# Householder tridiagonalisation of a 512 x 512 Laplacian: two dots in one sum, the step's vector operations reordered, and the pivot row summed early in the last block

## The reference, cut to what matters

```python
deg = jnp.sum(A, axis=0) + jnp.sum(A, axis=1) - jnp.diagonal(A)
d_inv_sqrt = jnp.where(deg > 0, jax.lax.rsqrt(deg), 0.0)
L = jnp.diag(deg) - A
L_norm = d_inv_sqrt[:, None] * L * d_inv_sqrt[None, :]
_, U = jnp.linalg.eigh(L_norm)
agg = jnp.einsum('mn,bnd->bmd', U.T, features)
h = jax.nn.relu(agg @ W1 + b1)
out = h @ W2 + b2
return jnp.einsum('nm,bmd->bnd', U, out)
```

## Time and profile before

| what | value |
|---|---|
| median of 3 runs | 5796.45 us (5794.7 to 5798.84) |
| the profiled execution | 5797.87 us, of it the profiled span 5796.2 us |
| busy: PE, PEld | 3847.7 us (66%), 2559.1 us (44%) |
| busy: DVE, ACT | 4287.2 us (74%), 1342.6 us (23%) |
| mean granted TensorE clock | 0.655 of 2.4 GHz |
| from the first x to the last (L297 to L404) | 47.3 to 2522.5 us |

### The profile page before, as it was taken

One profiled execution on the slowest core, in us unless ns is written; L12 is line 12 of the kernel. 1 busy time (PEld: TensorE's weight loads), 2 busy tenths in 40 slices (PEclk: granted clock), 3 DMA queues, 4 the chain that ended last, 5 costly groups with the idle time before them and its releaser, 6 DMA issues. The chain is left out here.

```text
span 5796.2 us, 63099 instructions
## 1 busy us (share of the span) xinstructions
PE 3847.7 (66%) x12287; PEld 2559.1 (44%) x12287; DVE 4287.2 (74%) x24282; ACT 1342.6 (23%) x5439; POOL 51.2 (1%) x82
## 2 busy tenths in 40 slices
PE   5889998898777777754445444441056687885757
PEld 5777777777655566641112111220033343322334
DVE  7999988888888877789999999999923312223354
ACT  1222222222322333310000000000002225333444
POOL 0000000000000000000000000000000000000000
PEclk6555555555555555567677677665568898997979
DMA  0000000000000000000000000000010000000000
GB/s 8 1 1 1 1 1 1 1 1 1 1 1 1 1 1 1 1 1 0 0 1 0 0 0 0 0 1 0 0 38 12 0 0 0 0 0 0 0 9 20
DMA packets 14148, 16.01 MB, mean 3 GB/s; under 512 B 571, under 2 KB 10214, under 8 KB 13798
## 3 DMA queue, kind: packets, MB, share of 16 engines
q1 hardware_dynamic: 13798, 12.48, 0.8%
HBM read 8.28 MB, written 4.19 MB: 2 GB/s over the span
## 5 line engine op out<-in xcount | busy, mean ns | idle before, releaser
L552 DVE RECIPROCAL sturm_recip<-sturm_pivots 128x32 f32<-128x32 f32 x2560 | 713.8, 320 | 0.0
L550 DVE SCALAR_TENSOR_TENSOR sturm_pivots<-sturm_recip,neg_e,ps 128x32 f32<-128x32 f32 x2560 | 470.3, 203 | 29.3 <-PE ps L502 29.3
L277 ACT ACTIVATE vectors<-V,refl 128x4 f32<-128x4 f32 (+3 forms) x511 | 152.6, 299 | 1218.0 <-DVE refl L394 1218.0
L510 PE MATMUL ps<-sturm_flags,ident_flags 128*128 128x512 bf16 x160 | 82.7, 621 | 522.8 <-ACT sturm_flags L525 522.8
L219 PE MATMUL ps<-dot_part,ones 128*128 128x1 f32 x766 | 224.3, 362 | 271.8 <-DVE dot_part L389 271.4
L219 PEld LDWEIGHTS ps<-dot_part,ones 128*128 128x128 f32 x766 | 191.6, 311 | 428.9 <-DVE dot_part L389 428.9
L208 PE MATMUL ps<-ident,vectors 128*128 128x128 f32 x1148 | 341.9, 435 | 33.3 <-DVE vectors L404 4.7
L1236 PE MATMUL ps<-h_features,WihT 128*128 x504 | 296.0, 747 | 49.3 <-ACT gates_skip L1267 28.3
L525 ACT ACTIVATE sturm_flags<-sturm_pivots,pivot 128x1024 bf16<-128x1024 f32 x80 | 91.8, 1148 | 1007.1 <-DVE pivots_mark L555 953.1
L501 PE MATMUL ps<-points,ident 128*128 128x512 f32 x320 | 250.8, 879 | 63.5 <-DVE points_mark L536 63.5
L510 PEld LDWEIGHTS ps<-sturm_flags,ident_flags 128*128 128x128 bf16 x160 | 10.5, 110 | 589.2 <-ACT sturm_flags L525 589.2
(11 more groups left out here) (461 smaller groups left out, 9356.9 us busy)
## 6 DMA issues: line engine op xcount, KB each, us to landing
out_dram<-x SPq DMA_DIRECT2D x16, 256.0 KB, 2.3
adj<-in_adj_dram SPq DMA_DIRECT2D x1, 1024.0 KB, 5.3
l2w_in<-in_L_gnn_W_dram SPq DMA_DIRECT2D x2, 128.0 KB
Wqkv<-in_L_gnn_Wqkv_dram SPq DMA_DIRECT2D x1, 192.0 KB
L_gnn_W<-in_L_gnn_W_dram SPq DMA_DIRECT2D x2, 64.0 KB
L_gnn_Wg<-in_L_gnn_Wg_dram SPq DMA_DIRECT2D x2, 64.0 KB
x<-in_x_dram SPq DMA_DIRECT2D x4, 0.5 KB
L_gnn_Wo<-in_L_gnn_Wo_dram SPq DMA_DIRECT2D x1, 64.0 KB
```

The costliest lines, as they stand in the source:

```text
L550: r.inc(nc.vector.scalar_tensor_tensor(out=S,in0=R,scalar=neg_e2[:,row+dr:row+dr+1],in1=XD[h%2][dr][:,slot],op0=ALU.mult,op1=ALU.add))
L552: r.inc(nc.vector.reciprocal(R,S))
```

## The change

In `tridiagonalise`, and in the helpers that say when tiles are updated:

- **One sum for both dots.** V.y and V.cc are two L389-like operations into `dp[:,0:2]`, summed by one matmul (`dots`). kappa = S (V.cc) + V.y is one operation. L221, L328 and L329 go.
- **Scalars.** The copy of the squared norm (L274) goes. One three-fold reciprocal of two products (L370, L371) and A1 (L359) becomes a reciprocal of N2 = S (S + alpha) and S; x_scaled multiplies by two column scalars at once. In blocks 1 to 3 V is made of `hs` = sub times sign and of T2.
- **Order.** p moves from ahead of the next x to behind it (`close`, blocks 0 to 2). y is made ahead of cc in blocks 0 to 2, behind it in block 3. The reciprocal, the sign, T2 and the corrections have an order of their own in each block. Where an instruction waits for several semaphores, the waits come in another order.
- **Sums.** For m < 256 the norm and the pairs' dots are one matmul over `gp`, behind ROWS; from 256 on the norm's sum waits for kappa and no longer for w.
- **Last block.** The pivot's row for step m+1 is summed behind the dot of step m, from bu and p. Its entry for w is then put in by VectorE in PSUM (`KAPH`, `row_at`). bu is made by VectorE there.
- **Updates.** One tile a step at most. In blocks 0 and 1 a step with an update has no product on TensorE, and VectorE multiplies all columns. Blocks 2 and 3 take the new version after 4 and 3 steps, not 2. ScalarE copies the updated tile ahead of its wait for beta (`u_ready`).

```diff
+def panel_lag(p): return (5,4,4,3)[panel_block(p)]
+def update_from(p): return (1,1,2,2)[panel_block(p)]
 def version(m):
...
+    p=m//PANEL-1
+    if p<0: return None
+    t=panel_block(p)+m%PANEL-update_from(p)
+    return (p,t) if m%PANEL>=update_from(p) and t<NT else None
+def products(m):
+
+    return sum(1 for q in range(1,m+1) if pe_tiles(q))
+def pe_tiles(m):
+
+    b=m//P
+    if b==NT-1: return range(NT-1,NT)
...
-                        nc.tensor.matmul(NORM[:,0:1],ones[:],nrm[:],start=True,stop=True).then_inc(s2_ps,1)
-                        nc.tensor.matmul(ROWS[:,X_:hi],at,XG[:,b,X_:hi],start=True,stop=True).then_inc(sel_ps,1)
-                        if L:
+                        if m>=SEP:
+                            pe.wait_ge(nrm_ready,m); pe.wait_ge(kap_ready,m-1)
+                            nc.tensor.matmul(NG[:,0:1],ones[:],gp[:,0:1],start=True,stop=True).then_inc(s2_ps,1)
+                        if m>1: pe.wait_ge(ub_ready,m-1); pe.wait_ge(w_ready,m-1)
+                        nc.tensor.matmul(ROWS[:,X_:last_slot(m)],pivot(m),XG[:,b,X_:last_slot(m)],start=True,stop=True).then_inc(sel_ps,1)
+                        if m<SEP:
+                            pe.wait_ge(nrm_ready,m)
+                            if m>1: pe.wait_ge(kap_ready,m-1); pe.wait_ge(gp_ready,m-1)
+                            nc.tensor.matmul(NG,ones[:],gp[:],start=True,stop=True).then_inc(s2_ps,1)
+                        else:
                             pe.wait_ge(gp_ready,m-1)
-                            nc.tensor.matmul(by_kind(gdot(m))[:,:,L[0]:L[1]],ones[:],gp[:,:,L[0]:L[1]],start=True,stop=True).then_inc(g_ps,1)
+                            nc.tensor.matmul(pair_dots(m),ones[:],halves(gp),start=True,stop=True).then_inc(g_ps,1)
...
-                        nc.tensor.matmul(DOT[:,0:1],ones[:],dp[:],start=True,stop=True).then_inc(dot_ps,1)
-                        pe.wait_ge(c_ready,m)
-                        nc.tensor.matmul(AT,at,XG[:,b,Y_:Y_+2],start=True,stop=True).then_inc(at_ps,1)
+                        nc.tensor.matmul(dots(m),ones[:],dp[:],start=True,stop=True).then_inc(dot_ps,1)
...
+                        if m==TAIL: pe.wait_ge(kap_ready,m-1)
+                        nc.tensor.matmul(NG[:,0:2],xx,XG[:,NT-1,E_:X_+1],start=True,stop=True).then_inc(s2_ps,1)
+                        pe.wait_ge(ub_ready,m-1); pe.wait_ge(w_ready,m-1)
+                        nc.tensor.matmul(pair_dots(m)[:,:,L[0]:L[1]],xx,by_kind(XG[:,NT-1,:])[:,:,L[0]:L[1]],start=True,stop=True).then_inc(g_ps,1)
...
+                        nc.tensor.matmul(dots(m),V[:,NT-1,m-1:m].broadcast_to([P,P]),XG[:,NT-1,Y_:Y_+2],start=True,stop=True).then_inc(dot_ps,1)
+                    if TAIL<=m+1<N:
+                        pe.wait_ge(ub_ready,m); pe.wait_ge(pc_ready,m)
+                        nc.tensor.matmul(ROWS[:,PC_:last_slot(m+1)],pivot(m+1),XG[:,NT-1,PC_:last_slot(m+1)],start=True,stop=True).then_inc(sel_ps,1)
...
                         act.wait_ge(x_ready,m)
-                        nc.scalar.activation(sq[:,u,sl],XG[:,sl,X_],ACT.Square,accum_out=nrm[:]).then_inc(nrm_ready,1)
-                    if m>PANEL and m%PANEL==1: rows_copied(m//PANEL-1)
+                        nc.scalar.activation(sq[:,2,sl],XG[:,sl,X_],ACT.Square,accum_out=gp[:,0:1]).then_inc(nrm_ready,1)
+                    if new_rows and m<SEP: rows_copied(m//PANEL-1)
                     act.wait_ge(s2_ps,m)
...
                     if TAIL<=m+1<N: nc.scalar.copy(XG[:,NT-1,E_:E_+1],ident[:,(m+1)%P:(m+1)%P+1]).then_inc(e_ready,1)
+                    if not wide:
+                        act.wait_ge(h_ready,m-TAIL+1)
+                        nc.scalar.activation(hs[:,sl],sub[:,sl,i],ACT.Copy,scale=s[:,u,H:H+1]).then_inc(hs_ready,1)
+                    if new_rows and m>=SEP: rows_copied(m//PANEL-1)
+                    if update_tile(m): tile_copied(*update_tile(m))
                     act.wait_ge(u_ready,m)
-                    nc.scalar.activation(XG[:,sl,U_],V[:,sl,i],ACT.Copy,scale=s[:,u,T0:T0+1]).then_inc(ub_ready,1)
+                    if wide: nc.scalar.activation(XG[:,sl,U_],V[:,sl,i],ACT.Copy,scale=s[:,u,T0:T0+1]).then_inc(ub_ready,1)
+                    act.wait_ge(ub_ready,m)
+                    nc.scalar.activation(ubh[:,sl],XG[:,sl,U_],ACT.Copy,scale=-0.5).then_inc(ubh_ready,1)
                     nc.scalar.copy(tau[:,i:i+1],s[:,u,T0:T0+1]).then_inc(kept,1)
                     nc.scalar.copy(esub[:,i:i+1],s[:,u,S_:S_+1]).then_inc(kept,1)
-                    act.wait_ge(ub_ready,m)
-                    nc.scalar.activation(ubh[:,sl],XG[:,sl,U_],ACT.Copy,scale=-0.5).then_inc(ubh_ready,1)
-                    for p,t in updated_tiles(m): tile_copied(p,t)
...
+                def close(q):
+
+                    w=q%2; sl=slice(q//P,NT); early=TAIL<=q+1<N
+                    col=lambda j: s[:,w,j:j+1]
+                    v.wait_ge(dot_ps,q)
+                    nc.vector.scalar_tensor_tensor(out=col(KAP),in0=col(S_),scalar=dots(q)[:,1:2],in1=dots(q)[:,0:1],op0=ALU.mult,op1=ALU.add).then_inc(kap_ready,1)
+                    if q<TAIL: p_col(q)
+                    v.wait_ge(ubh_ready,q)
+                    if q>=PANEL and q%PANEL==0: v.wait_ge(gt_ps,q//PANEL)
+                    v.wait_ge(pc_ready,q)
+                    if early:
+                        v.wait_ge(kap_ready,q)
+                        k.inc(nc.vector.tensor_scalar(col(KAPH),col(KAP),-0.5,None,ALU.mult)); half_at=k.at()
+                        v.wait_ge(sel_ps,q+1)
+                    v.wait_ge(kap_ready,q)
+                    nc.vector.scalar_tensor_tensor(out=XG[:,sl,G_+SPREAD+slot(q)],in0=ubh[:,sl],scalar=col(KAP),in1=XG[:,sl,PC_],op0=ALU.mult,op1=ALU.add).then_inc(w_ready,1)
+                    if early:
+                        v.wait_ge(ds,half_at)
+                        k.inc(nc.vector.scalar_tensor_tensor(out=ROWS[:,G_+SPREAD+slot(q):G_+SPREAD+slot(q)+1],in0=col(KAPH),scalar=ROWS[:,G_+slot(q):G_+slot(q)+1],in1=ROWS[:,PC_:PC_+1],op0=ALU.mult,op1=ALU.add)); row_at[0]=k.at()
+                def p_col(q):
+                    sl=slice(q//P,NT)
+                    v.wait_ge(y_ready,q); v.wait_ge(c_ready,q)
+                    nc.vector.scalar_tensor_tensor(out=XG[:,sl,PC_],in0=XG[:,sl,C_],scalar=s[:,q%2,S_:S_+1],in1=XG[:,sl,Y_],op0=ALU.mult,op1=ALU.add).then_inc(pc_ready,1)
...
+                        if b==0:
+                            after("S")
+                            mark("V",nc.vector.scalar_tensor_tensor(out=V[:,sl,i],in0=sub[:,sl,i],scalar=col(S_),in1=x,op0=ALU.mult,op1=ALU.add))
+                        else:
+                            if wide: after("T2","hs")
+                            else: v.wait_ge(hs_ready,m-TAIL+1); after("T2")
+                            mark("V",nc.vector.scalar_tensor_tensor(out=V[:,sl,i],in0=hs[:,sl],scalar=col(T2),in1=x,op0=ALU.mult,op1=ALU.add))
...
+                    def dot_parts():
+                        v.wait_ge(y_ready,m); after("V")
+                        k.inc(nc.vector.tensor_tensor_reduce(out=sq[:,0,sl],in0=V[:,sl,i],in1=y,scale=1.0,scalar=0.0,op0=ALU.mult,op1=ALU.add,accum_out=dp[:,0:1]))
+                        v.wait_ge(c_ready,m)
+                        nc.vector.tensor_tensor_reduce(out=sq[:,1,sl],in0=V[:,sl,i],in1=cc,scale=1.0,scalar=0.0,op0=ALU.mult,op1=ALU.add,accum_out=dp[:,1:2]).then_inc(dp_ready,1)
+                    def denominator():
+                        after("S")
+                        mark("N2",nc.vector.scalar_tensor_tensor(out=col(N2_),in0=col(S_),scalar=ALPHA,in1=col(S_),op0=ALU.add,op1=ALU.mult))
...
+                        after("xym"); v.wait_ge(u_ready,m)
+                        mark("xt",nc.vector.tensor_scalar(xt[:,sl],xym[:,sl,0],col(T0),col(Q),ALU.mult,ALU.mult))
...
+                        if L:
+                            v.wait_ge(ub_ready,m-1); v.wait_ge(x_ready,m); v.wait_ge(w_ready,m-1)
+                            link(nc.vector.tensor_tensor(prod[:,sl,:,0:n],pairs(),x.unsqueeze(2).unsqueeze(3).broadcast_to([P,NB,2,n]),ALU.mult))
+                            nc.vector.tensor_reduce(halves(gp)[:,:,L[0]:L[1]],prod[:,sl,:,0:n].rearrange("p t e s -> p e s t"),AX.X,ALU.add).then_inc(gp_ready,1)
+                        v.wait_ge(A_copied,copies_of(version(m))); v.wait_ge(xrow_ps,m)
+                        if b==0:
+                            multiply(2); inverse(); sign(); multiply(1); twice_norm(); multiply(2)
+                            by_dots(); by_rows(); shift(); add_product(); corrections(); reflector()
+                            matrix_times_x(); column_of_A()
+                        elif b==1:
+                            multiply(3); sign(); inverse(); signed_sub(); by_dots(); twice_norm(); by_rows()
+                            add_product(); corrections(); reflector()
+                            matrix_times_x(); column_of_A(); shift()
+                        else:
```

(54 more changed lines are left out.)

201 lines of the change are left out of this document (61 added, 140 removed).

## The result

The changed kernel takes 5712.14 us (median of 4 runs, 5709.32 to 5713.75), the kernel before, beside it, 5795.57 (4 runs, 5794.57 to 5798.84): a ratio of 0.9855 [0.9843, 0.9868]. The change saves 83 us where I had forecast 179; the range, 5555 to 5700, does not hold the result. The profiled execution took 5713.75, its span 5712.1, and the mean granted clock was 0.656 (0.655 before).

The account below looks back on a forecast made before the run. In the 511 Householder steps VectorE's chain of tiny dependent operations was taken as the bound, with some TensorE waits. Blocks 0 to 3 gain 35 + 44 + 67 + 33 = 179 us, giving 5618 us, range 5555 to 5700.

Parts of the forecast that it names:

- the price of the hand-overs behind several waits: Between dependent operations: w to prod 0.28 us with the blocking wait last; 0.03 for two waits ahead of x.
- Block 2: Steps of block 2: 0.48 us a step from front and middle less a longer tail, plus update-step effects; 67 us.
- The tail of 1.32: Block 2, from y to the next x: 1.32 us against 1.29 before, with the second dot and x_scaled added.
- Block 0: Steps of block 0: 0.25 us a step over 127 steps, and 3 us for the rest; 35 us.
- the update steps would come out even: Block 0's update steps: VectorE's full last tile, at most 0.4 us more, offset by an addition dropped and an earlier update.
- Block 1: Steps of block 1: 0.27 us a step, 35 us, plus 9 us in update steps; 44 us.
- Block 3: Steps of block 3: y at 2.02 to 2.05 us after x, x at 3.16; 0.26 a step, 33 us.
- The covers: Blocks 0 and 1, ScalarE: the updated tile's copy is done at 4.5 us, ahead of beta near 5.
- Only the number of operations counts: Rival for all steps: VectorE operations at 0.2 us each, less longer update-step products; gain 39 us, 5759; chance 0.05.
- The gates in blocks 0 and 1: Rival: w or the parts 0.3 us later hold the root; blocks 0 and 1 gain nothing; 5698 us; chance 0.12.
- The clock: Slower rival, stages behind the steps: TensorE granted under 0.77; at 0.70, 180 us longer, at 0.67, 5890; chance 0.03.
- the one with 0.04: Rival, no change: waits put their issue time on the chain, 0.35 us a step, leaving 5797; chance 0.04.

Follow-up runs that it names:

- experiment 1: The changed kernel with the wait that ends last moved to the front of each list, except at KAPH; same operations: 5622.3 us, ratio to before 0.9695.
- experiment 2: The changed kernel with the two waits ahead of x exchanged, so that y_scaled's, which ends last, is written second: 5745.49 us.
- Experiment 4: The changed kernel with the last tile's product back on TensorE in update steps too, in blocks 0 and 1: 5701.77 us.
- experiment 6: From experiment 1, block 3's pivot row summed behind the pairs' dots of its own step, without KAPH and the entry set in PSUM: 5660.56 us.
- experiments 1 and 7: The second of these: from experiment 1, x_scaled multiplied by one column scalar, leaving out 1/S, so output isn't the reference's: 5593.37 us.

## Why the prediction was wrong

**The step that failed** is the price of the hand-overs behind several waits. Where the prediction names it, in the front of a step, it says: "From w to prod it was 0.31, more than a link of 0.25; with the blocking wait last I take 0.28". I took a late wait at the end of the list for the cheaper place. It is the dear one: 0.35. At x_scaled, at S of block 3 and behind the transposes the prediction added nothing for the waits and took a bare link. The table has the distance from the start of an operation to the start of the one that waits for it, by the place of that wait in the source:

| place of the late wait | seen at | start to start, us |
|---|---|---|
| first | x behind y_scaled; w to prod in experiment 1 | 0.25; 0.26 |
| middle of three | w to prod before; p to w after | 0.31; 0.31 |
| last of three; last of two | w to prod after; x behind y_scaled in experiment 2 | 0.35; 0.31 |

The change wrote the late wait last at prod, the first product, x_scaled, by_rows, KAPH and S of block 3 and, on TensorE, the joined sum and the pairs' dots of block 3. Moving all of them but KAPH's (experiment 1) was worth 90 us. It left 4 of the 94 us between my forecast and the result, the net of 9 us that block 2 had over and what the other blocks lacked.

**Block 2** (67 forecast, 47 measured, 76 in experiment 1). Taken over the 16 steps with m mod 8 = 6, prod is at 0.95, the first product 1.29, y 2.86 and x 4.20 in the changed kernel (forecast 0.83, 1.17, 2.72, 4.04) and at 0.81, 1.15, 2.73 and 3.99 in experiment 1. The middle is right to 0.02. The tail of 1.32 measured 1.34, but by two errors: x stands 0.25 behind y_scaled and not 0.28, and x_scaled 0.27 behind the reciprocal and not 0.21, with its late wait last. The turn behind an update gave 9 us (forecast 11), and the longer pending pairs took 4 (forecast 5).

**Block 0** (35, 12, 32.5). The steps of block 0 with m mod 8 = 6, from step 17 on, fell from 5.73 to 5.64, 0.09 where 0.25 was laid out, and to 5.46 in experiment 1. Products behind the transposes began at 1.55 (1.46 before): the first product has its late wait last, 0.15 behind the end of the transposes (1.40), and 0.04 behind it in experiment 1. Here "the earlier w gains nothing" was right and hid a loss. The tail measured 1.42, not 1.32: with four columns the dots are 0.12 apart and the first stands 0.15 behind cc. That the update steps would come out even held, from step 17 on: they gained 0.14, 0.09, 0.11 and -0.02. Experiment 4 shows that it was a poor standard, since with the product on TensorE three of them are 0.25 to 0.31 shorter.

**Block 1** (44, 16, 43). The steps with m mod 8 = 6 stayed as they were, 4.85 and 4.87, and are 4.63 in experiment 1. The steps with m mod 8 from 1 to 4, the update steps and the one behind them, gave nearly the whole gain, 15.9 of 16.2 us (forecast for update steps 9). The joined sum's weight load begins 0.12 behind the parts (1.50 after 1.38) and the reciprocal comes at 2.48, 0.09 behind the end of the products; in experiment 1 these are 0.05, 2.31 and 0.03. The tail holds S as well (the order of block 1 puts it behind y), which I had left out: 1.44.

**Block 3** (33, 5.5, 23.5). KAPH, the pairs' dots and S, as shown above. What experiment 1 lacks in this block, 9.5 us, has the size of KAPH's hand-over: it stands 0.34 behind kappa where a link is 0.25, so w starts at 0.59 and not at 0.52, and 0.07 a step would be 9 us. In experiment 1 it stands at 0.35 still, but that edit did not free it: since kappa's wait is written a second time behind the others, the packed trace of step 452 has a semaphore instruction that waits for kappa from 2152.86 to 2152.91, and KAPH starts at 2152.96. In experiment 6, where w has KAPH's place and kappa's wait last, w starts at the same 0.35. So 0.34 is the table's price for a last wait. That KAPH would come down to 0.25 with kappa's wait in front alone was not tried.

**The covers** held: in step 60 the update (L195) ran from 2.24 to 4.15 after x and its copy to 4.74, ahead of the reciprocal pair that beta comes from, at 5.55.

**The rivals.** Only the number of operations counts (5759): fell. Independent and dependent operations with a column scalar stand 0.13 and 0.25 apart after the change too, and experiments 1 and 7 moved 90 and 29 us at an equal number of operations. The Trainium skill says beside it ("VectorE: DVE Perf Modes", section "The DRAIN you can't avoid") that chained operations took the same time with a semaphore behind each as with one at the end. No run here tries that, since the number of waits stayed as it was but for KAPH. What the runs add is that the place of a wait in its list is not free: 90 us. The gates in blocks 0 and 1 (5698, near the result in number): there is one, in block 1, where the reciprocal comes 0.09 behind the products. Experiment 1 has the same gate, at 0.03, and gained 43 us there. The clock: 0.76 behind the steps after 0.77. The prediction called this a sign of the slower outcome, but the stretch was not longer (3270 us after 3274). Nearest in mechanism was the one with 0.04: "the waits [...] each put their issue time on the chain". It was priced at 0.35 a step by their count; what the runs price is their order, and it took 90/511 = 0.18.

## What to carry to other kernels

Where an operation waits for several things, write the wait that ends last first, and look in the trace which that is: it differs between stages and can change with an edit ahead of it, so a change that adds waits is not priced until their order is. Before a hand-over is made shorter, find the chain beside it; if that is as long, as L221 here, nothing comes of it. When an extra operation is given to an engine "because it is even", try the steps apart, as in block 0 the first step behind a panel and the others had different answers.
